# Moving the cast of a weight matrix within ScalarE's image step, and the gate's exponent behind the copies of turned images

## The reference

```python
x = relu(x + softplus(s) * bn(conv1x1(relu(bn(conv3x3(relu(bn(conv1x1(x)))))))))
t = tokens(x)                                  # 16 images, 196 tokens, 256 channels
n = layernorm(t)
q, k, v = split(n @ w_qkv)                     # 16 heads of 16
context = softmax(q * scale, -1)^T-weighted with softmax(k, tokens)
t = t + (context applied to v) @ w_out + b_out
f = layernorm(t)
probs = softmax(f @ gate_w + gate_b); top 2 of 8 experts, weights normalised
t = t + sum over the two: weight * (gelu(f @ w1[e] + b1[e]) @ w2[e] + b2[e])
```

## Time and profile before

| what | value |
|---|---|
| median of 3 runs | 717.31 us (716.01 to 720.59) |
| the profiled execution: time, span | 722.2 us, 720.4 us |
| busy share of the span: PE, PEld, DVE, ACT, POOL | 85%, 76%, 64%, 44%, 30% |
| casts L480 | 16, each 1.88 to 1.91 us |
| rests L1111 on VectorE | 14, each 2.28 to 2.29 us |

### The profile page before, as it was taken

The page is one execution under the profiler, slowest core; times in us unless marked ns, Lnnn a source line. Parts: engine busy times, 40 slices in busy tenths (PEclk is TensorE's granted clock), DMA queues, the critical chain, the costliest instruction groups (busy, mean ns, idle before and its releaser), DMA issues.

```text
span 720.4 us, 13755 instructions
## 1 busy us (share of the span) xinstructions
PE 613.9 (85%) x3884; PEld 545.1 (76%) x3884; DVE 462.2 (64%) x1500; ACT 319.6 (44%) x625; POOL 217.6 (30%) x193
## 2 busy tenths in 40 slices
PE   6664589999989985328999999999999999999982
PEld 3553478888878864317999999999999899999972
DVE  1788869999998775514655655655655655655650
ACT  1634578887776532103333433433433433433430
POOL 5230222324555564630212212222122221221221
PEclk9875689999999986559999999999999999999996
DMA  9480679879897862241247383643825628422211
GB/s 272 140 330 21 238 287 350 303 286 310 310 317 263 341 253 61 80 122 24 41 103 245 46 300 57 213 132 61 286 45 163 186 44 269 85 39 46 31 16 15
DMA packets 50517, 121.23 MB, mean 168 GB/s; under 512 B 7564, under 2 KB 39184, under 8 KB 44304
## 3 DMA queue, kind: packets, MB, share of 16 engines
q1 hardware_dynamic: 30704, 98.62, 37.8%
q0 software_dynamic: 11136, 14.00, 11.5%
q10 hardware_dynamic: 8608, 7.73, 4.1%
HBM read 68.22 MB, written 52.11 MB: 167 GB/s over the span
## 4 chain that ended last, share of the span: by engine, by line
PE 65%; DVE 17%; issue 5%; ACT 4%; DMA 4%; SPq 2%; another core or an unknown queue 1%; DVEq 0%; POOL 0%; ACTq 0%; POOLq 0%
PE ps L847 44%; PE ps L874 6%; DMA wset<-in_ew 3%; PE ps L684 2%; DVE wset L1111 2%; PE ps L741 2%; PE ps L674 2%; PE ps L840 2%; PE ps L771 1%; PE ps L730 1%; DVE bst L992 1%; PE ps L762 1%; DVE stt L1022 1%; ACT wset L480 1%; PE ps L778 1%
## 5 line engine op out<-in xcount | busy, mean ns | idle before, releaser
L464 POOL DMA_INDIRECT out<-ys,xr x56 | 86.7, 1548 | 308.8 <-DVE ys L1381 235.0
L847 PE MATMUL ps<-wset,hTh 128*128 x896 | 162.5, 282 | 3.5 <-DVE hTl L1349 3.5
L847 PEld LDWEIGHTS ps<-wset,hTh 128*128 128x128 f32 x896 | 141.1, 189 | 10.1 <-issue 5.7
L847 PE MATMUL ps<-wset,xrTh 128*128 x448 | 147.1, 410 | 0.0
L640 ACT ACTIVATE hb<-hb 128x512 f32<-128x512 f32 x112 | 70.3, 633 | 134.4 <-DVE hb L1370 134.4
L847 PE MATMUL ps<-wset,hTl 128*128 x448 | 126.1, 281 | 0.0
L646 ACT CAST hTh<-ps 128x512 fp32r<-128x512 f32 x112 | 60.3, 590 | 98.4 <-PE ps L874 97.9
L1376 DVE TENSOR_TENSOR yb<-ps,bset 128x256 f32<-128x256 f32 x56 | 23.8, 425 | 123.6 <-PE ps L847 123.6
L847 PEld LDWEIGHTS ps<-wset,xrTh 128*128 128x128 f32 x448 | 81.0, 191 | 15.7
L847 PE MATMUL ps<-wset,xrTl 128*128 x224 | 89.2, 398 | 0.0
L1370 DVE TENSOR_TENSOR hb<-ps,bset 128x512 f32<-128x512 f32 x112 | 75.5, 685 | 18.5 <-PE ps L847 18.5
(11 more groups left out here) (189 smaller groups left out, 963.8 us busy)
## 6 DMA issues: line engine op xcount, KB each, us to landing
split_weights<-wset SPq DMA_DIRECT2D x16, 2048.0 KB
wset<-split_weights SPq DMA_DIRECT2D x32, 1024.0 KB
wset<-in_ew SPq DMA_DIRECT2D x16, 1024.0 KB, 11.1
xr<-rows_by_expert ACTq DMA_DIRECT2D x56, 132.5 KB, 2.2
bset<-in_eb SPq DMA_DIRECT2D x8, 640.0 KB
img<-in_x SPq DMA_DIRECT2D x8, 392.0 KB, 6.5
out<-img SPq DMA_DIRECT2D x16, 196.0 KB
rows_by_expert<-padrow SPq DMA_DIRECT2D x9, 132.5 KB
```

The lines of the kernel that those rows point to most:

```text
L464: pool.indirect_dma_start(out, bass.IndirectOffsetOnAxis(xr[:, r % XR, C + E:ROW].bitcast(U32), 0), ys[:, r % YS, :], None, compute_op=ALU ...
L847: last = pe.matmul(dst, rows_k[:, k * 128:(k + 1) * 128], wset[:, bass.ds(column(k) + rest, width)], start=(k == 0 and n == 0), stop=(k == ...
```

## The change

In ScalarE's loop of image steps, `split_leading` moves from the end of step n, ahead of the copies of transposed images (in the first three steps: behind them), to the middle of step n + 1, behind the two `in_relu` and ahead of the copy of turned key exponents. The matrix that is cast for VectorE's rest of step n is so cast in step n itself. `route_exp` moves from ahead of the two copies of transposed images to behind them. The constant `FILL` goes. Nothing changes in the lists of the other engines, and no instruction is added or removed.

```diff
-FILL = 3
...
             for n in range(SLOTS_A):
-                for stage, do in (("soft", soft_v), ("soft", soft_exps), ("in", in_relu),
-                                  ("soft", soft_kT), ("norm2", lambda i: norm2_norm(i, n)),
-                                  ("norm", lambda i: norm_norm(i, n)), ("in", in_keep), ("ctx", ctx_proj)):
+                for stage, do in (("soft", soft_v), ("soft", soft_exps), ("in", in_relu)):
+                    if 0 <= n - LAG[stage] < B:
+                        do(n - LAG[stage])
+                if EARLY <= n - 1 + EARLY < UNITS:
+                    split_leading(n - 1 + EARLY)
+                for stage, do in (("soft", soft_kT), ("norm2", lambda i: norm2_norm(i, n)),
+                                  ("norm", lambda i: norm_norm(i, n)), ("in", in_keep), ("ctx", ctx_proj),
+                                  ("norm", norm_xT), ("norm2", norm2_xT)):
                     if 0 <= n - LAG[stage] < B:
                         do(n - LAG[stage])
                 if n >= ROUTE_LAG and n % 2 == 0 and (n - ROUTE_LAG) // 2 < B // 2:
                     route_exp((n - ROUTE_LAG) // 2)
-                if FILL <= n < UNITS - EARLY:
-                    split_leading(n + EARLY)
-                for stage, do in (("norm", norm_xT), ("norm2", norm2_xT)):
-                    if 0 <= n - LAG[stage] < B:
-                        do(n - LAG[stage])
-                if n < FILL:
-                    split_leading(n + EARLY)
```

## The result

The changed kernel takes 732.3 us (median of 730.93 to 733.49) against 717.2 for the kernel before: a ratio of 1.0173, 95% interval 1.0138 to 1.0208 (the quotient of the two medians is 1.021). The forecast was 720.7, its range ended at 726.0. The profiled execution of the changed kernel took 732.82 us with a span of 731.0. In the file after, ScalarE's lines have a number smaller by one and those of TensorE and VectorE one smaller by three (L1108 is the rest, L1148 the first instruction behind the gate's exponent, L727 the products of q).

A forecast was written before the change was run, and what follows sets the result against it. VectorE, without waits in steps 5 to 11, was taken as the limit. Terms -3.1 + 3.7 + 1.3 - 1.15 + 1.2 + 1.5 = +3.45 moved 717.31 to 720.7 us; range 713.5 to 726.

The forecast's parts named there:

- Load at the start, -3.1: Steps 2 to 4: ScalarE no longer waits for matrix 4's load, so step 4's statistics start 3.1 us earlier.
- Cast behind the relus, 0.62 a step: Steps 5, 6, 7, 9, 11, 13: VectorE's rest waits for the later cast, 0.62 each, 3.7 us in all.
- Steps 12 and 14, -1.15: Earlier turned images remove VectorE's waits behind TensorE there, gaining 0.7 and 0.45 us, together 1.15.
- Exponent in the tail, +2.7: From step 15 on: VectorE waits for the later exponent, costing 1.2 us in step 16 and 1.5 in step 20.
- the third rival: Steps 3 and 4: short waits drop TensorE to its lower clock, costing 2.8 us; 723.5 us, chance 0.13.
- the count of ScalarE's list: Even steps: instructions counted from VectorE's second mix without waits put the exponent's result at 7.01, costing 0.67 us a step.
- The 0.5 by which L1151 was to wait in every odd step: Expected profile sign: VectorE's L1151 waits about 0.5 us for the exponent in every odd step from 9 to 21.
- the exponent in steps 8 and 10: VectorE waits for the exponent behind the copies: 1.3 us for both steps, the cast's 0.18 each included.
- The first two rivals: First: cast off the path shortens VectorE's steps, 712.8 us, chance 0.15; second: delays wash out, 717.3 to 719, chance 0.12.

The follow-up runs named there:

- the kernel with one cast moved: Kernel before with only the cast of matrix 4 moved behind the relus of step 3; 718.1 us, ratio 1.0018.
- cast-only kernel: Kernel before with only the casts moved behind the relus, the gate's exponent staying ahead of the copies of transposed images; ratio 1.0080.
- with the exponent late in the tail: Changed kernel with the exponent back ahead of the copies in steps 8 to 14 only; 724.1 us, ratio 1.0105.
- the added products: Changed kernel with unused TensorE products ahead of turned key exponents and context in odd steps from 9 on; 724.8 us, ratio 1.0118.
- hybrid: Kernel before with the casts of matrices 2 to 6 only moved behind the relus, exponent unmoved; 714.1 us, ratio 0.9942.
- after_tail_early: Changed kernel with the exponent back ahead of the copies in steps 16 to 22 only; 728.1 us, ratio 1.0154.
- before_again: Second execution of the kernel before, nothing changed; 716.82 us.

## Why the prediction was wrong

**Load at the start, -3.1: right in size.** Step 4's statistics start at 95.16 (95.6 was forecast), and rest 4 starts 3.46 earlier than in the profiled execution of before. The working named one wait; the gain needs the next cast away too, as the kernel with one cast moved shows.

**Cast behind the relus, 0.62 a step: right in mechanism, some 1 us too small in all.** From rest 4 to rest 8 the cast-only kernel takes 43.22, the kernel before (second execution) 40.85: 2.37 in four steps, 0.59 each. VectorE does wait for the cast in steps 5 to 8, by 0.42 to 0.53. From rest 8 to rest 14 it loses 72.87 - 69.62 = 3.25, where three odd steps and three even ones by my terms make 3 x 0.62 + 3 x 0.18 = 2.4. Step 8, an even one, had been given 0.18 too.

**Steps 12 and 14, -1.15: not there.** The wait of 1.37 was that execution's own: the second one waits 0.54 and 0.38 in these steps, which take 1.77 less there, over a third of the 4.9 us by which the profiled one lay above the median. With the cast alone moved they take 11.50 and 11.47, no less than in the second execution.

**Exponent in the tail, +2.7: right as far as the rows can tell.** The waits for it in steps 17, 19 and 21 are 0.90, 1.40 and 0.45 in the cast-only kernel and 2.67, 0.84 and 1.96 with the exponent late in the tail: +1.77, -0.56 and +1.51, where 1.7, 0 and 1.5 were forecast; the load comes 2.0 later than with the cast alone and 3.8 later than in the second execution of before, counted from rest 14. The two executions without the late exponent differ by 1.8 themselves.

**The step that failed: TensorE's clock, and with it the exponent in steps 8 to 14.** I wrote "Whether TensorE keeps up here is a matter of its clock" and asked it of steps 3 and 4 alone; the third rival stands there too, with 2.8 us and a chance of 0.13. In the odd steps from 9 on I took TensorE's slack as harmless, because VectorE was full: "a wait added to a list that has none is paid in full, and a wait elsewhere is not". TensorE's wait was paid. Its waits there were several and short, 0.80 ahead of v and 0.38 ahead of the context in step 11 of before; with v no longer late and the key maximum later, they collect ahead of the key exponents. Behind them the level falls, with q at 3.62 behind 1.65 and 0.74 of idle time. The section of the Trainium skill that the prediction cites (TensorE: Matmul & The Clock Gate, section on HAM oscillation) has the mechanism, a wait behind which the next burst starts at the lower clock, but the waits of its example are 3 to 5 us long; here shorter ones did it, and the measurement decides. The same error sits in the count of ScalarE's list: it gave the exponent's end at 7.01 behind the second mix on the ground that the copies ahead of it wait for nothing. In step 8, before the level falls, L1148 starts 7.16 behind the mix. In step 10 the mix starts at 167.09 and L1148 at 175.86, 8.77 later, because copies ahead of it wait for a TensorE that is late, the first transposed image 1.08. With the added products it is 7.16 again in step 10 (173.76 - 166.60): the count was right, but for a TensorE that keeps its level. The 0.5 by which L1151 was to wait in every odd step was 0.20 in step 9 and 0.87 to 1.17 in the next three.

Against the second execution of before the first load comes 15.75 later, and the terms add up to it: -0.85 up to rest 8; +3.25 for the cast and +6.06 for the exponent up to rest 14 (78.93 = 69.62 + 3.25 + 6.06; for the exponent in steps 8 and 10 the forecast had 1.3, the cast's 0.18 each included); and 95.86 - 88.57 = 7.29 behind it. Of the 6.06, 5.20 hang on the clock. The split of the 7.29 is not shown. By one order of the kernels 1.79 are there with the cast alone, 2.03 are the exponent in the tail, and 3.47 come with the exponent of the middle steps, behind which q of step 15 takes 3.60. By the other order nothing is left for the middle: the kernel with the exponent early in the tail only has q at 3.40 in step 15 and needs 88.45, in an execution 4.0 us below its median, and the hybrid with q at 3.57 needs 88.69. So that the 3.47 is the clock of step 15 is not shown either. The 1.79 is the clock in step 18, which varies between executions of the kernel before as well; I can't put it down to the cast.

The first two rivals are out: VectorE's steps did not get shorter, and the delays did not wash out. The side on which the time lay was the forecast's, and 5 to 7 of the 15.75 us came by its own terms (-0.85 + 3.25 + 0.86, and 2.0 to 3.8 in the tail). A further 5.2 were the third rival's mechanism in another place, at nearly twice its 2.8. What is left, 3.5 to 5.3 behind rest 14, no run assigns.

## What to carry to other kernels

Before calling an engine's slack free, ask where its idle time will lie after the change: several short waits that are gathered in one place can cost TensorE its clock, and then it is no longer the engine with slack. An instruction that is moved behind a copy takes over what the copy waits for, so the copies' own releasers belong into the count. And a wait that only one profiled execution shows is no gain to be booked; the distance of that execution to the median is the warning.

## What the hardware showed unexpectedly

TensorE fell to the lower level behind idle times of 1.65 and 0.74 with one short product between them (q at 3.62), and held the upper one behind 1.15 and 0.74 in the steps 9 to 15 of cast_only (1.89). But the length of these two waits does not decide alone: the level held once behind 1.70 and 0.74 (after_tail_early, step 13), and of two executions with some 0.7 and 0.7 in step 15 it held in one (before_again, 1.89) and fell in the other (hybrid, 3.57). What decides besides is open. More work for TensorE, 22 instructions in an odd step, made the changed kernel 7.5 us faster. And the executions of one unchanged kernel spread over 8 us (714.1 to 721.9 in one series); in the two that were profiled, most of the difference lay in TensorE's waits and levels in steps 12 to 19.
